# Four stages of a twelve-stage transformer kernel: expert products issued a block ahead, weights quantised two stages early, idle transposes on TensorE, context loads on another queue

## The chip, the cores and the metric

The kernel runs on one core of a Trainium2 chip. The metric is the device time of one launch in microseconds (us); the kernel before was timed three times. All times below are us unless marked ns.

## The reference

The input is x, 32 sequences of 64 tokens of width 128 (2048 tokens in all), a context of 32 sequences of 1601 keys of width 128, and masks over the keys. Four layers follow, each of a cross-attention, a mixer and a feed-forward part; every part adds to x what it computes from a layer norm of x. The change touches three of the twelve parts:

```
L1 ffn, routed experts (8 experts, hidden width 512)
    sim = x e^T; 7 best experts by sim; scores of normalised x and e, + 0.1
    weights = softmax of the two best scores, zero for the other experts
    out = sum over e of weights[e] * (gelu(x W1[e] + b1[e]) W2[e] + b2[e])

L2 xattn, many heads (16 heads of width 8)
    out = softmax(q k^T / sqrt(8), masked keys out) v, then W_o

L3 xattn, one head: softmax((x Wq + bq)(ctx Wk + bk)^T / sqrt(128), masked) (ctx Wv + bv)

L3 ffn, quantised
    Q(m): in blocks of 16, scale = max|m| / 6, |m| / scale rounded to
          the grid 0, .5, 1, 1.5, 2, 3, 4, 6, times sign(m) * scale
    out = Q(silu(Q(x) Q(Wg)^T) * (Q(x) Q(Wu)^T)) Q(Wd)^T
```

## The kernel before

Five engines run programs of their own, written out by hand, and one core does everything. x stays in on-chip memory as 16 tiles of 128 tokens. Each of the twelve parts is one Stage: its buffers live as long as the stage, and at its end all engines meet at a barrier (the profile shows TensorE's side of it as PEq L123). Inside a stage the engines are ordered by semaphores alone. Steps and RoundSteps are lists of step names from which the count is worked out that an engine must wait for, so the order of an engine's work is the order of the code in its block.

**Routed experts** (`routed_experts`). The routing comes first: similarities and norms on TensorE (L1769, L1772), the choice of experts on VectorE, one Exp on ScalarE (L1910), then `weights`, a table of 2048 x 8. TensorE turns it (L1778, 16 transposes) and multiplies it with b2 (L1787, 16 products), which VectorE adds to x. Then come 8 experts by 4 column blocks of 512 tokens, 32 blocks in all. A block is 4 first products of 128x512 (L1800, one for each bank of `ph`), 4 gelus on ScalarE (L1925), 16 second products in four sums of four (L1807, into one of two banks of `po`) and 4 weighted additions to x on VectorE (L1894). The program on TensorE is first, second, first, second. The second products need the block's last gelu, which needs the last of the first products. Every expert's b1 is copied to `b1e` by ScalarE, since the loop's expert index is a register. Weights come on the sync engine's (SP's) queue into two buffers.

**Many heads** (`many_head_cross_attention`). 32 sequences times 14 bundles (each a group of four heads and a part of the keys) give 448 bundles. TensorE's program is a list of steps b from -32 to 457. For b below 0 it prepares keys and values of the first sequences (K at L2975, V at L2971) and, from b = -18, starts the products for the maxima (L2907), 18 bundles ahead of their use (LEAD = 18). In a bundle proper it subtracts the maximum (L2920, L2923), in three bundles of every 14 also takes masked keys out (`less_out`, L2933; in the other eleven VectorE does it with a minimum, L3089), forms the scores (L2894) and three bundles later multiplies with V (L2954). From b = 430 there is nothing left to start for the maxima, and from 448 on only the last sums are finished (L2983 to L2988).

**One head** (`kept_cross_attention`). 16 rounds of two sequences. A round needs the context turned (`ctxT`, 2 x 800 KB), the context (`ctx`, 2 x 800 KB, in four transfers) and the mask, in three buffers each; SP issues them all in one program, mask, turned, then the context of the round before. A turned load waits for the score products of three rounds before (S3), a context load for the products that use it (M3). ScalarE does an Exp of 128x1601 and three copies in a round.

**Quantised layer** (`quantised_ffn`, `Quant`, `quant_vector`, `quant_scalar`). The weights, 128 x 1120 numbers (573 KB), are loaded at the stage's start and quantised by VectorE in 14 instructions (L2520 to L2547), with |y| and the sign of y on ScalarE (L2553 and the line after), y being the weights over their scale. TensorE then turns them (L2606, L2609), and only after copying the result does VectorE begin the layer norm of x. After it come the quantisation of x (`qx`) and, in four groups of 512 tokens, two products, a Silu, the quantisation of the product (`qh`) and the last product. ScalarE's |y| waits for VectorE's y (L2526), and VectorE's next instruction (L2528) waits for |y|.

## Time and profile before

| what | value |
|---|---|
| time, median of 3 | 3136.5 us (3125.68, 3136.5, 3137.94) |
| the profiled execution's own time | 3132.72 us |
| its span, mean granted TensorE clock | 3130.9 us, 0.905 |
| busy | PE 2645.0 (84%), PEld 1692.3, DVE 2029.6 (65%), ACT 1385.4 (44%), POOL 426.2 (14%) |
| DMA | 188.98 MB, mean 60 GB/s |
| largest groups | DVE L3043 544.7, PE L2907 496.4, PE L2894 463.5 (all many heads) |

PE is TensorE's products, PEld its weight loads, DVE VectorE, ACT ScalarE, POOL GpSimd, SP the sync engine, which mostly issues transfers. Busy shares are means over twelve stages with different limits. The stages' places in the span: routed experts 710.8 to 1015.2, many heads 1015.2 to 2262.1, one head 2646.2 to 2826.1 with a self-attention behind it, quantised layer from 2928.3 to the end. The granted clock is a share of 2.4 GHz: 1.00 is that level, 0.50 is the lower level of 1.2 GHz. The profiled execution is 3.8 us below the median.

### The profile page before, as it was taken

To read this page: it belongs to the slowest core of one execution; us is meant where nothing else is said; L and a number is where in the kernel's file an instruction comes from. 1 tells how busy PE (TensorE), PEld (TensorE's weight loads), DVE (VectorE), ACT (ScalarE), POOL (GpSimd) and SP (SyncE) were. 2 spreads that over 40 slices of the span, in tenths; PEclk is the share of its full clock that TensorE was granted. 3 is DMA by queue.
4 is the path that set the end of the run, shared out by engine and by line. 5 is a ranking of instruction groups with operands and counts; after the bars stand their busy time and mean duration, and the time that the engine had idled before them with its cause. 6 is when DMAs were issued, how large, how long until landed. Compare 5 with 4: busy or idle time off the path is not lost. (4 is left out here: it accounts for less than half of the span.)

```text
span 3130.9 us, 65894 instructions
## 1 busy us (share of the span) xinstructions
PE 2645.0 (84%) x26698; PEld 1692.3 (54%) x26698; DVE 2029.6 (65%) x6809; ACT 1385.4 (44%) x2527; POOL 426.2 (14%) x299
## 2 busy tenths in 40 slices
PE   7989555996998799999999999999847988988333
PEld 5767354554666355566555665555525555655223
DVE  5563324674111378999998999889468876436776
ACT  3441222663333145555555555555339953335411
POOL 0000120530000000000000000000006940544100
PEclk9989776997999589999999999999679999999766
DMA  7960420000000100000100001000012211990000
GB/s 247 332 209 1 134 58 7 2 3 15 21 14 9 38 33 23 23 23 23 33 23 23 23 23 33 23 23 2 9 30 68 95 41 52 332 335 9 8 0 14
DMA packets 73343, 188.98 MB, mean 60 GB/s; under 512 B 12130, under 2 KB 39717, under 8 KB 73008
## 3 DMA queue, kind: packets, MB, share of 16 engines
q1 hardware_dynamic: 72016, 182.91, 17.7%
q8 instruction: 212, 3.47, 0.5%
q0 software_dynamic: 1024, 1.85, 0.2%
q14 instruction: 91, 0.75, 0.1%
HBM read 154.19 MB, written 30.79 MB: 59 GB/s over the span
## 5 line engine op out<-in xcount | busy, mean ns | idle before, releaser
L3043 DVE CUSTOM_DVE_ANT_0 L_xattn_junk<-L_xattn_ps_mx,L_xattn_shift 128x512 f32<-128x512 f32 (+1 forms) x1024 | 544.7, 569 | 127.3 <-issue 117.8
L3124 ACT ACTIVATE L_xattn_pT<-L_xattn_ps_st 128x512 f32<-128x512 f32 x768 | 416.9, 594 | 412.4 <-PE L_xattn_ps_st L2894 412.4
L2907 PE MATMUL L_xattn_ps_mx<-L_xattn_kT,L_xattn_qb 32*128 32x512 f32 (+1 forms) x2048 | 496.4, 567 | 1.8 <-DVE L_xattn_tops L3043 1.8
L2894 PE MATMUL L_xattn_ps_st<-L_xattn_qb,L_xattn_kT 32*128 32x256 f32 (+1 forms) x3328 | 463.5, 389 | 0.0
L3089 DVE TENSOR_TENSOR L_xattn_pT<-L_xattn_pT,L_xattn_capT 128x512 f32<-128x512 f32 (+1 forms) x704 | 419.2, 636 | 40.5 <-ACT L_xattn_pT L3124 37.8
L2894 PEld LDWEIGHTS L_xattn_ps_st<-L_xattn_qb,L_xattn_kT 32*128 32x128 f32 (+1 forms) x3328 | 304.1, 183 | 20.6 <-issue 1.2
L2954 PE MATMUL L_xattn_ps_pv<-L_xattn_pT,L_xattn_v 128*17 128x128 f32 x6656 | 267.6, 280 | 0.0
L2954 PEld LDWEIGHTS L_xattn_ps_pv<-L_xattn_pT,L_xattn_v 128*17 128x17 f32 x6656 | 148.4, 98 | 167.0 <-issue 81.0
L2920 PE MATMUL L_xattn_ps_st<-L_xattn_less,L_xattn_ones_b 3*128 3x512 bf16 x768 | 180.7, 390 | 1.4 <-ACT L_xattn_pT L3124 1.2
L1894 DVE SCALAR_TENSOR_TENSOR x<-L_ffn_ps_o,L_ffn_weights,x 128x128 f32<-128x128 f32 x128 | 36.1, 344 | 224.2 <-PE L_ffn_ps_o L1807 224.2
L2907 PEld LDWEIGHTS L_xattn_ps_mx<-L_xattn_kT,L_xattn_qb 32*128 32x128 f32 x2048 | 157.8, 188 | 36.0 <-DVE L_xattn_tops L3043 23.5
L2861 POOL TENSOR_TENSOR L_xattn_qb<-ln_sq,L_xattn_four 128x256 f32<-128x256 f32 x32 | 19.6, 614 | 1105.1 <-PE L_xattn_ps_st L2894 1085.9
L1925 ACT ACTIVATE L_ffn_gelu<-L_ffn_ps_h,L_ffn_b1e 128x512 f32<-128x512 f32 x128 | 87.9, 687 | 163.1 <-PE L_ffn_ps_h L1800 159.7
L1807 PEld LDWEIGHTS L_ffn_ps_o<-L_ffn_w,L_ffn_gelu 128*128 128x128 f32 x1024 | 116.7, 192 | 51.4 <-ACT L_ffn_gelu L1925 51.4
L1807 PE MATMUL L_ffn_ps_o<-L_ffn_w,L_ffn_gelu 128*128 128x128 f32 x1024 | 122.8, 278 | 24.9 <-ACT L_ffn_gelu L1925 24.9
L2971 PE MATMUL L_xattn_ps_prep<-L_xattn_wv,L_xattn_ctxT 128*128 128x128 f32 (+1 forms) x832 | 132.2, 300 | 2.3 <-ACT L_xattn_kT L3137 2.3
L2975 PE MATMUL L_xattn_ps_prep<-L_xattn_ctxT,L_xattn_wk 128*128 128x512 f32 (+1 forms) x256 | 130.1, 592 | 3.1 <-ACT L_xattn_v L3140 2.0
L2971 PEld LDWEIGHTS L_xattn_ps_prep<-L_xattn_wv,L_xattn_ctxT 128*128 128x128 f32 (+1 forms) x832 | 105.2, 196 | 40.4 <-issue 33.1
L2920 PEld LDWEIGHTS L_xattn_ps_st<-L_xattn_less,L_xattn_ones_b 3*128 3x128 bf16 x768 | 45.3, 91 | 135.4 <-ACT L_xattn_pT L3124 75.5
L1800 PE MATMUL L_ffn_ps_h<-xnT,L_ffn_w 128*128 128x512 f32 x256 | 117.2, 601 | 0.0
L2242 ACT ACTIVATE L_attn_xs<-L_attn_xiT,L_attn_bt 128x256 f32<-128x256 f32 x256 | 105.2, 493 | 0.0
L3431 POOL TENSOR_SCALAR L_xattn_out_keys<-L_xattn_mask 128x1536 bf16<-128x1536 uint8 x16 | 78.7, 4919 | 184.6 <-DMA L_xattn_mask<-in_mask_pairs 168.6
(612 smaller groups left out, 4952.9 us busy)
## 6 DMA issues: line engine op xcount, KB each, us to landing
...
L_xattn_out_keys<-scratch_q SPq DMA_DIRECT2D x32, 200.1 KB, 10.0
L_ffn_w<-in_L_ffn_w SPq DMA_DIRECT2D x4, 1024.0 KB, 10.5
...
```

The lines of the kernel that those rows point to most:

```text
L1800: nc.tensor.matmul(ph[:, k, :], w1[:, u, P * k:P * k + P], c.xnT[:, 512 * i:512 * i + 512], start=True, stop=True).then_inc(PE.did(f"h{i}{ ...
L1807: last = nc.tensor.matmul(po[:, i % 2, P * j:P * j + P], g[:, i % 2, k, P * j:P * j + P], w2[:, u, k, :], start=(k == 0), stop=(k == FC - 1))
L2242: last = nc.scalar.mul(xs[:, k % 2, j, :], xiT[:, t, :], bt[:, t, n:n + 1])
L2894: last = nc.tensor.matmul(st[0:chunk[j], w % 3, 256 * c2:256 * c2 + 256], kT[n % 3][r:r + 32, P * j:P * j + chunk[j]], qb[n % 3][r:r + 32, ...
L2907: last = nc.tensor.matmul(mx[:, w % 3, to:to + width], qb[n % 3][32 * g:32 * g + 32, 2 * (p % 2):2 * (p % 2) + 2, :].rearrange("p h q -> p ...
L2920: nc.tensor.matmul(st[:, w % 3, :], ones_b[r:r + 3, :], less[n % 2][r:r + 3, :, :].rearrange("p c k -> p (c k)"), start=True, stop=False, ...
L2954: last = nc.tensor.matmul(pv[32 * q:32 * q + 17, P * half:P * half + P], v[n % 3][0:chunk[j], j, 4 * half + q, :], pT[b % HELD][0:chunk[j] ...
L2971: last = nc.tensor.matmul(prep[0:chunk[j], to:to + P], ctxT[:, n % 2, P * j:P * j + chunk[j]], wv[:, :], start=True, stop=True)
L2975: last = nc.tensor.matmul(prep[:, 0:width], wk[:, :], ctxT[:, n % 2, 512 * m:512 * m + width], start=True, stop=True)
L3043: last = nc.vector.tensor_tensor_reduce(out=junk[:, w % 3, to:to + width], in0=mx[:, w % 3, to:to + width], in1=shift[:, k0:k0 + width], s ...
L3089: nc.vector.tensor_tensor(x, x, capT[0:k, j[0]:j[1], :].unsqueeze(2).broadcast_to([k, j[1] - j[0], 4, S]), ALU.min)\
L3124: nc.scalar.activation(pT[b % HELD][:, :, gi, :], st[:, w % 3, :].rearrange("p (c k) -> p c k", c=2), ACT.Exp)\
```

## The change

1. **Routed experts.** The blocks are numbered n = 0 to 31. TensorE issues the first products of block n+1 ahead of the second products of block n. The two steps that need `weights` (its turns and the products with b2) become `second_bias` and stand ahead of the second products of block 2; so the first products of blocks 0 to 3 and the second of 0 and 1 stand before it. ScalarE does the gelus of blocks 0 to 2 before the routing's Exp. The products with b2 go to the banks of `turn`. All indices are constants, and b1e with its copies is gone.
2. **Many heads, lead-in and end.** `kept_busy(b)` puts transposes of the identity, whose result nobody reads, behind each step of TensorE's program: 8 in each of the 14 steps -32 to -19, 6 in each of the 18 steps -18 to -1, 4 in each of the 27 steps 431 to 457, the last ones behind one wait at b = 431. Masked keys in the last 18 bundles (three with `less_out` before) are left to VectorE.
3. **One head.** The context loads move from SP's queue to ScalarE's: 12 transfers ahead of its layer norm, and four behind its copies in each of the rounds 1 to 13. SP keeps the masks and the turned loads.
4. **Quantised weights.** They get buffers that live over the last three stages. SP issues their load in the one-head stage's round 1; ScalarE takes |w| and sign(w) in round 3; VectorE does one step of the quantisation in each of the rounds 3 to 15. In the quantised layer TensorE's turns start at once.
5. **Quant.** ScalarE takes |m| and sign(m) of the source itself, not of y, and VectorE multiplies |m| by 1/scale in place; the buffer y is gone.

```diff
@@ routed_experts, tensor engine
-                        for k in range(FC):
-                            ...
-                            nc.tensor.matmul(ph[:, k, :], w1[:, u, P * k:P * k + P], c.xnT[:, 512 * i:512 * i + 512],
-                                             start=True, stop=True).then_inc(PE.did(f"h{i}{k}"), 1)
-                        pe.wait_ge(*A.at(f"g{i}{FC - 1}", e))
...
+            first(0)
+            for n in range(BLOCKS):
+                if n + 1 < BLOCKS:
+                    first(n + 1)
+                if n == AHEAD - 1:
+                    second_bias()
+                second(n)
@@ routed_experts, scalar engine
+            act.wait_ge(loaded, 80)
+            for n in range(AHEAD):
+                gelu(n)
             act.wait_ge(*V.at("gap"))
             nc.scalar.activation(ex[:, :], gap[:, :], ACT.Exp).then_inc(A.did("exp"), 1)
...
+            for n in range(AHEAD, BLOCKS):
+                gelu(n)
@@ many_head_cross_attention
-        masked_here = lambda b: b % ROUND in ON_TENSOR
+        masked_here = lambda b: b % ROUND in ON_TENSOR and b < BUNDLES - LEAD
...
+            def kept_busy(b):
+
+                if b < 0:
+                    for _ in range(8 if b < -LEAD else 6):
+                        nc.tensor.transpose(st[:, 2, 0:P], c.ident[:, :], c.ident[:, :])
+                elif b > BUNDLES - LEAD:
+                    if b == BUNDLES - LEAD + 1:
+                        pe.wait_ge(topped, 2 * BUNDLES)
+                    for _ in range(4):
+                        nc.tensor.transpose(mx[:, 0, 0:P], c.ident[:, :], c.ident[:, :])
@@ kept_cross_attention, sync engine, then vector and scalar engine
-                if r >= 1:
-                    if r >= 4:
-                        sp.wait_ge(*PE.at(f"M3_{r - 4}"))
-                    load_context(r - 1)
+                if r == 1:
+                    sp.dma_start(ahead.w[:, :], a[f"{ahead_name}_w"]).then_inc(ahead.loaded, 16)
...
+                quantised_ahead(c, dve, ahead, r)
...
+            for r in range(3):
+                load_context(r)
             ln_scalar(c, act, V, A, PE, tp)
...
+                if 1 <= r < NT - 2:
+                    load_context(r + 2)
+                if r == FIRST_AHEAD:
+                    act.wait_ge(ahead.loaded, 16)
+                    nc.scalar.activation(ahead.q.ay[:, :], ahead.w[:, :], ACT.Abs).then_inc(ahead.signed, 1)
+                    nc.scalar.activation(ahead.q.sign[:, :], ahead.w[:, :], ACT.Sign).then_inc(ahead.signed, 1)
@@ quant_vector, quant_scalar, quantised_ffn
-    nc.vector.tensor_tensor(blocks(q.y[:, :]), blocks(src), wide(q.rscale), ALU.mult).then_inc(*step("y"))
     dve.wait_ge(*A.at(f"{tag}_abs", t))
+    nc.vector.tensor_tensor(blocks(q.ay[:, :]), blocks(q.ay[:, :]), wide(q.rscale), ALU.mult).then_inc(*step("ay"))
...
-    act.wait_ge(*V.at(f"{tag}_y", t))
-    nc.scalar.activation(q.ay[:, :], q.y[:, :], ACT.Abs).then_inc(A.did(f"{tag}_abs"), 1)
-    nc.scalar.activation(q.sign[:, :], q.y[:, :], ACT.Sign).then_inc(A.did(f"{tag}_sign"), 1)
+    c.nc.scalar.activation(q.ay[:, :], src, ACT.Abs).then_inc(A.did(f"{tag}_abs"), 1)
+    c.nc.scalar.activation(q.sign[:, :], src, ACT.Sign).then_inc(A.did(f"{tag}_sign"), 1)
...
-            pe.wait_ge(*V.at("w_out"))
...
-            dve.wait_ge(loaded, 16)
-            quant_vector(c, dve, qw, V, A, "w", 0, w[:, :], w[:, :])
```

`quantised_ahead` holds the same arithmetic as quant_vector, a step for each round:

```
    step = r - FIRST_AHEAD                      # FIRST_AHEAD = 3
    0: scale = max|w|      1: scale / 6         2: 1 / scale
    3: |w| * (1/scale)     4: a = 2 (|y| > 5), b = |y| > 1.75
    5, 6: a += |y| > 3.5, 2.5                   7, 8, 9: b += |y| > 1.25, 0.75, 0.25
    10: a += b / 2         11: a *= sign        12: w = a * scale
```

The order of TensorE's program from the end of the routing's products, before (L1778 and L1787 turn the weights and multiply b2, L1800 are first products, L1807 second):

```order
L1772 MATMUL L_ffn_ps_turn<-L_ffn_emb,L_ffn_ones 128x8
L1778 MATMUL L_ffn_ps_turn<-ident,L_ffn_weights 8x128 x16
L1787 MATMUL L_ffn_ps_o<-L_ffn_b,L_ffn_weightsT 128x128 x16
L1800 MATMUL L_ffn_ps_h<-xnT,L_ffn_w 128x512 x4
L1807 MATMUL L_ffn_ps_o<-L_ffn_w,L_ffn_gelu 128x128 x16
```

And now (L1782 are first products, L1792 second, L1802 and L1811 the weights' turns and b2):

```order
L1773 MATMUL L_ffn_ps_turn<-L_ffn_emb,L_ffn_ones 128x8
L1782 MATMUL L_ffn_ps_h<-xnT,L_ffn_w 128x512 x8
L1792 MATMUL L_ffn_ps_o<-L_ffn_w,L_ffn_gelu 128x128 x16
L1782 MATMUL L_ffn_ps_h<-xnT,L_ffn_w 128x512 x4
L1792 MATMUL L_ffn_ps_o<-L_ffn_w,L_ffn_gelu 128x128 x16
L1782 MATMUL L_ffn_ps_h<-xnT,L_ffn_w 128x512 x4
L1802 MATMUL L_ffn_ps_turn<-ident,L_ffn_weights 8x128 x16
L1811 MATMUL L_ffn_ps_turn<-L_ffn_b,L_ffn_weightsT 128x128 x16
L1792 MATMUL L_ffn_ps_o<-L_ffn_w,L_ffn_gelu 128x128 x16
```

16 first products and 32 second ones now stand between the norms and the weights' turns, and a block's second products have the next block's first products ahead of them.

The lead-in of the many-head stage on TensorE, before (K at L2975, V at L2971, products for the maxima at L2907):

```order
L2975 MATMUL L_xattn_ps_prep<-L_xattn_ctxT,L_xattn_wk 128x65
L2971 MATMUL L_xattn_ps_prep<-L_xattn_wv,L_xattn_ctxT 65x128
L2907 MATMUL L_xattn_ps_mx<-L_xattn_kT,L_xattn_qb 128x512 x2
L2975 MATMUL L_xattn_ps_prep<-L_xattn_ctxT,L_xattn_wk 128x512
L2907 MATMUL L_xattn_ps_mx<-L_xattn_kT,L_xattn_qb 128x512 x4
```

And now (L3002 are the idle transposes, L2982, L2978 and L2914 the three of before):

```order
L2982 MATMUL L_xattn_ps_prep<-L_xattn_ctxT,L_xattn_wk 128x65
L3002 MATMUL L_xattn_ps_st<-ident 128x128 x16
L2978 MATMUL L_xattn_ps_prep<-L_xattn_wv,L_xattn_ctxT 65x128
L3002 MATMUL L_xattn_ps_st<-ident 128x128 x40
L2914 MATMUL L_xattn_ps_mx<-L_xattn_kT,L_xattn_qb 128x512 x2
L2982 MATMUL L_xattn_ps_prep<-L_xattn_ctxT,L_xattn_wk 128x512
L3002 MATMUL L_xattn_ps_st<-ident 128x128 x6
L2914 MATMUL L_xattn_ps_mx<-L_xattn_kT,L_xattn_qb 128x512 x2
```

Nothing of before has moved there; the transposes stand between, 112 ahead of the first product for the maxima and 108 behind it.

A round of the one-head stage on ScalarE now (L3602 is the Exp, L3608 the copies, DMA rows its new issues; before, only the first two stood here, and the four DMA rows stood on SP between the turned loads and the next mask):

```order
L3602 ACTIVATE L_xattn_sc,L_xattn_rows<-L_xattn_sc,L_xattn_bias 128x1601 [waits L3_xattn_vector_steps]
L3608 COPY L_xattn_probsT<-L_xattn_ps_turn 128x512 [waits L3_xattn_tensor_steps] x3
L3590 DMA L_xattn_ctx<-in_ctx 128x1536
L3592 DMA L_xattn_ctx<-in_ctx 65x128
L3590 DMA L_xattn_ctx<-in_ctx 128x1536
L3592 DMA L_xattn_ctx<-in_ctx 65x128
```

The next round's Exp stands behind the four issues.

## Rows read from the trace of the kernel before

**Rows 1.** Stretches: length; busy (instructions) of PE, PEld, DVE, ACT, POOL; clock; DMA share, GB/s
```profile
1042.10:1117.50 75.40, 69.18 (x165) 30.37 (x165) 23.42 (x128) 9.75 (x19) 0.00 (x0) 0.50 0.06 22
...
2676.00:2678.00 2.00, 2.00 (x8) 0.59 (x6) 1.59 (x4) 0.00 (x0) 0.00 (x0) 0.50 0.13 40
2760.00:2770.00 10.00, 8.17 (x87) 5.68 (x85) 3.78 (x20) 3.18 (x5) 5.44 (x3) 1.00 1.02 344
```

**Rows 2.** Timeline of PE, expert loop: start, length, engine, line, output<-inputs, records, [idle before <-releaser]
```profile
861.17 3.60 PE L1800 MATMUL L_ffn_ps_h<-xnT,L_ffn_w 128*128 128x512 f32 x8
865.55 3.84 PE L1807 MATMUL L_ffn_ps_o<-L_ffn_w,L_ffn_gelu 128*128 128x128 f32 x32 [0.78 <-ACT L_ffn_gelu L1925]
869.22 3.60 PE L1800 MATMUL L_ffn_ps_h<-xnT,L_ffn_w 128*128 128x512 f32 x8
```

**Rows 3.** Timeline of PE, routed experts, from the norms to the first block
```profile
729.53 0.57 PE L1772 MATMUL L_ffn_ps_turn<-L_ffn_emb,L_ffn_ones 128*128 128x8 f32 x2
745.00 3.46 PE L1778 MATMUL L_ffn_ps_turn<-ident,L_ffn_weights 128*8 128x128 f32 x16 [14.89 <-DVE L_ffn_weights L1877]
...
754.47 5.62 PE L1800 MATMUL L_ffn_ps_h<-xnT,L_ffn_w 128*128 128x512 f32 x8
```

**Rows 4.** Timeline of ACT, the same stretch
```profile
742.76 0.22 ACT L1910 ACTIVATE L_ffn_ex<-L_ffn_gap 128x16 f32<-128x16 f32 x1 [8.25 <-DVE L_ffn_gap L1860]
...
756.65 1.28 ACT L1925 ACT_TABLE_LOAD   x1 [7.35 <-PE L_ffn_ps_h L1800]
```

**Rows 5.** Timeline of PE, lead-in of the many-head stage
```profile
1042.12 2.08 PE L2975 MATMUL L_xattn_ps_prep<-L_xattn_ctxT,L_xattn_wk 128*128 128x512 f32 x2 [1.11 <-ACT L_xattn_capT L3114]
1044.87 2.07 PE L2971 MATMUL L_xattn_ps_prep<-L_xattn_wv,L_xattn_ctxT 128*128 128x128 f32 x8 [0.68 <-ACT L_xattn_kT L3137]
...
1060.23 2.08 PE L2907 MATMUL L_xattn_ps_mx<-L_xattn_kT,L_xattn_qb 32*128 32x512 f32 x4
```

**Rows 6.** Timeline of PE, idle transposes that the L0 ffn stage already has (L1569)
```profile
393.43 3.91 PE L1569 MATMUL L_ffn_ps_h<-ident 128*128 128x128 f32 x20 [27.40 <-DMA scratch_in<-xn,L_ffn_to]
397.18 1.04 PE L1576 MATMUL L_ffn_ps_turn<-ident,L_ffn_slots 128*128 128x128 f32 x8
```

**Rows 7.** Timeline of PE, end of the many-head stage
```profile
2205.93 0.46 PE L2920 MATMUL L_xattn_ps_st<-L_xattn_less,L_xattn_ones_b 3*128 3x512 bf16 x2
...
2225.06 0.61 PE L2920 MATMUL L_xattn_ps_st<-L_xattn_less,L_xattn_ones_b 3*128 3x512 bf16 x2
...
2228.29 0.61 PE L2920 MATMUL L_xattn_ps_st<-L_xattn_less,L_xattn_ones_b 3*128 3x512 bf16 x2
...
2254.85 2.76 PE L2954 MATMUL L_xattn_ps_pv<-L_xattn_pT,L_xattn_v 128*17 128x128 f32 x48
```

**Rows 8.** Timeline of DVE, the weights' quantisation: its first and its last instruction
```profile
2932.17 1.32 DVE L2520 TENSOR_REDUCE L_ffn_qw_scale<-L_ffn_w 128x70 f32<-128x1120 f32 x1 [4.12 <-DMA L_ffn_w<-in_L_ffn_w]
...
2947.85 1.32 DVE L2547 TENSOR_TENSOR L_ffn_w<-L_ffn_qw_a,L_ffn_qw_scale 128x1120 f32<-128x1120 f32 x1
```

**Rows 9.** Waits of the last 206 us: who waits for whom, us, times, longest
```profile
DVE L_ffn_qh_a L2528 <- ACT L_ffn_qh_ay L2553: 5.8, 4, 1.4
...
DVE L_ffn_qx_a L2528 <- ACT L_ffn_qx_ay L2553: 2.0, 1, 2.0
```

**Rows 10.** Timeline of SP (its issues), one-head stage
```profile
2654.46 0.44 SPq L3408 DMA_DIRECT2D L_xattn_ctx<-in_ctx  x1
...
2760.59 1.33 SPq L3408 DMA_DIRECT2D L_xattn_ctx<-in_ctx  x1
2761.96 3.22 SPq L3410 DMA_DIRECT2D L_xattn_ctx<-in_ctx  x1
2765.22 0.82 SPq L3408 DMA_DIRECT2D L_xattn_ctx<-in_ctx  x1
2766.09 1.19 SPq L3410 DMA_DIRECT2D L_xattn_ctx<-in_ctx  x1
...
2770.58 1.74 SPq L3408 DMA_DIRECT2D L_xattn_ctx<-in_ctx  x1
```

More of the change, by code:

```diff
@@ L1772, in _ @@
             nc.tensor.matmul(tp[1][:, 0:E], ones[:, :], emb2[:, :], start=True, stop=True).then_inc(PE.did("te"), 1)
-            pe.wait_ge(*V.at("weights"))
-            for i in range(4):
-                if i >= 2:
-                    pe.wait_ge(*(A if i % 2 else V).at(f"wT{i - 2}"))
-                for j in range(4):
-                    last = nc.tensor.transpose(tp[i % 2][0:E, P * j:P * j + P], weights[:, 4 * i + j, :], c.ident[:, :])
-                last.then_inc(PE.did(f"wT{i}"), 1)
@@ L2567, in quantised_ffn @@
         nc, a = c.nc, c.a
-        w = s.sb("w", [P, 2 * IP + I])
+        w = ahead.w
         wguT = s.sb("wguT", [P, 2, IP])
```

252 lines of the change are left out of this document (152 added, 100 removed).

## The prediction, made before the changed kernel had run

> **What bounds the kernel now.** Read the stretches first [rows 1]: engines, granted clock and DMA show a different limit in each stage. In the lead-in of the many-head stage TensorE is busy for 69.18 of 75.40 us at clock 0.50: it is the bound, at half speed. In the one-head stage, in ten us, DMA is saturated (share 1.02, 344 GB/s) while VectorE works 3.78 and ScalarE 3.18: transfers are the bound. Then read the timelines. In the expert loop TensorE is the bound but for a wait of 0.78 for the last gelu in each block [rows 2]; before the loop it idles 14.89 for the routing's table [rows 3]. In the quantised layer VectorE works through the weights from 2932.17 to 2949.17 (2947.85 + 1.32), 4.12 after it began to wait for them [rows 8], and everything stands behind it. The waits between engines come last [rows 9]. So all five parts of the change lie on the path, and each is priced in its own stage.
>
> **Expert loop.** A block takes 8.05 (861.17 to 869.22), of which the second products, started at 865.55, take 3.67 [rows 2]. The first products take 8 records of 0.43 = 3.44. With them a block ahead, the gelu runs beside 3.67 of second products and the wait of 0.78, with 0.16 of draining, goes: 7.11 a block. Now the start. The last product of the norms ends at 730.1 [rows 3]. There blocks 0 to 3's first and 0 and 1's second products begin at once, the first block at the low clock (5.4, by the 5.62 at 754.47 [rows 3]), the others 3.44 and 3.67: 5.4 + 3 x 3.44 + 2 x 3.67 = 23.0, end 753.1. The routing on VectorE runs beside it. Its Exp was at 742.76 and the table ready at 745.00, 2.2 later [rows 3, 4]. Now ScalarE still has gelus to do until about 747, then a table load of 1.28 [rows 4], so the table comes at about 750.5, still covered. The turns and the products with b2 took 9.5 (745.00 to 754.47), partly at the low clock; I take 8. Then 30 second and 28 first products: 30 x 3.67 + 28 x 3.44 = 206.4. I add 2.1 for block 2's and 3's sums, which on VectorE stand behind four b2 additions, and 2 for a slower clock after it (5.62 against 3.44 is 2.2). End: 753.1 + 8 + 2.1 + 206.4 + 2 = 971.6. Before it was 754.47 + 2.2 + 32 x 8.05 = 1014.3. **-42.7**, 29 of it from the 31 waits of 0.94, 14 from the start. Bounds: -29 if the start gains nothing, -47 without the two additions. The weights' transfers of an expert have four blocks to land in; the eight copies of b1 went beside TensorE.
>
> **Lead-in of the many heads.** Two halves: preparation from 1042.12 to 1060.23, 18.1, with waits of 0.68 between units [rows 5], and the rest to 1117.50, 57.3, all at 0.50 [rows 1]. A transpose costs 0.20 in the row of 20 at the low clock (3.91) and 0.13 in the next, 8 in 1.04 [rows 6]; that row ends warm, so for one at the low clock I take 0.24, a little under twice 0.13. First half now: a key unit of 2.0 and the first two groups of eight (3.4) at or near the low clock, then five units at 1.04, two of 0.35, and 12 groups of eight at 1.04, which fill the waits: 5.4 + 5.2 + 0.7 + 12.5 = 23.8, **+5.7**. Second half at full clock: 57.3 / 2 = 28.6, plus 18 x 6 x 0.13 = 14.0, is 42.6, **-14.7**. The first bundles, which before still ran at the low clock, give 1: **-10** in all. Bounds: -15 (57.3 + 18.1 halved, plus 28.6 of transposes, less waits filled) and 0, if the clock falls back for a part of it.
>
> Here a rule and a row disagree. The row: 20 transposes of the identity, alone after 27.40 of idling, were followed by transposes at 0.13 each [rows 6], so the clock rose under transposes. The Trainium skill, page "TensorE: Matmul & The Clock Gate", section "Part 4: PE-mode transpose", says that the full clock does not engage for transposes, which do not count as busy in the way products do. By that rule the added work would be pure loss, the rival R2 below, and the sum 3104 in place of 3046. I go by the row, with a doubt: in that stretch a DMA ran too, and in the lead-in products mixed with waits stayed at 0.50 although TensorE was busy 92% of the time.
>
> **End of the many heads.** From b = 431 at 2205.93 to the last sums at 2254.85 is 48.9 [rows 7]. The first bundles take 1.8, then the clock is low and a bundle takes 3.23 (2225.06 to 2228.29), with `less_out` 4.5 to 5. Now, warm: 13 bundles of 1.82, four short ones of 1.23, 17 x 4 transposes of 0.13 (8.8), and about 2 of waiting for a gap in ScalarE or for VectorE's minimum: 39.4. Ten more steps add 5.2 of transposes, which lie in the waits of the last sums, at a doubled speed: +1.3. **-8.** Bounds: -14 without the waits, and +15, the case R1.
>
> **Quantised layer.** The stage started its wait at 2928.05 (2932.17 - 4.12), and the weights were out at 2949.17 [rows 8]: 21.1, less 0.3 for what now has to start cold, -20.8. VectorE's waits for |y| were 2.0 for x and 5.8 in four groups [rows 9]; |m| is now taken beside the block maxima: -7.8. **-28.6.** Bounds: -25 to -29.
>
> **One head.** VectorE's 13 steps of at most 1.32 [rows 8] and ScalarE's two of some 1.2 fit into rounds of 10, in which they are busy 3.8 and 3.2 [rows 1]. On ScalarE 12 issues stand ahead of the layer norm: 12 x 0.44 [rows 10] = +5.3. The context's third load, which waited on SP behind a turned load, now fills the hole at 2676 (40 GB/s [rows 1]): 1.64 MB at 344 GB/s is 4.8, less what moved in it: -4.6. The weights add 573 KB, 1.7. **+2.4.** Behind each round's copies ScalarE issues four transfers, and who waits for that is its next Exp. On SP the four took 1.33 + 3.22 + 0.82 + 1.19 = 6.56 in a round of 9.99 (2760.59 to 2770.58) [rows 10]. ScalarE has 10.0 - 3.2 = 6.8 for them, 1.7 each. That hides them, but by little. I take them to be shorter there, near the 0.44, since SP's queue held mask and turned loads too. Bounds: -4 to +34.
>
> **Sum:** -42.7 - 10 - 8 - 28.6 + 2.4 = -86.9, against the profiled execution's own 3132.7: 3045.8, say **3046**. By the median of the runs, 3.8 higher, it would be 3050.
>
> **The rivals.**
> - **R1, the clock falls at the end of the many heads.** A bundle with waits for ScalarE may lose it as at 2215. Then 22 steps pay 4 x 0.24 = 21, five pay 0.5, three `less_out` (1.5 each) go: +15 to +17 instead of -8. About 3070. For it: TensorE waits for ScalarE's exps and the clock did fall there. Against: the transposes fill just these waits. 0.16.
> - **R2, the lead-in stays at 0.50.** 220 transposes of 0.24 are 53, less 5 for the waits they fill: +48 instead of -10, 3104. For it: 69.18 of 75.40 busy at 0.50 [rows 1]. Against: rows 6. 0.08. The rule of the skill's Part 4 gives this case.
> - **R3, ScalarE's queue.** If an issue costs 1.7 to 2.1 there, the start pays 12 x 1.26 = 15 up to 12 x 1.66 = 20 more, and 13 rounds pay 4 x 2.1 - 6.8 = 1.6 each, 21: between +15 and +41, about 3074. For it: SP's own 6.56. 0.13.
> - **R4, slower than before:** the same place, but each of the issues takes 3.22, the dearest of SP's [rows 10]. 13 x (12.9 - 6.8) = 79, and 12 x 2.78 = 33 at the start: 3158. It is slower by over 0.5% from a mean issue of 3.1 on. Against: no round of SP came near. 0.01.
> - **R5, the first change doesn't do what it says:** the second products still find no gelu ready, because ScalarE's four gelus (a wait of their own for the bank that the second products two blocks ago read) start late. 31 x 0.94 = +29, 3075. Against: 3.67 of cover. 0.03.
>
> **How the numbers follow.** The forecast has 0.59; its own range is 3032 to 3064 by the bounds. To hold 8 in 10 I need R1, most of R3 and R5: 3033 to 3084. A measurement of this kernel tells 0.5% (15.7 us) from no change. Every case but R4 is faster by more than that; two of the rivals together (R2 with R3 or R1) come to 3128 to 3132: faster 0.97, same 0.02, slower 0.01.
>
> **What would show it.** In the profile after: blocks of 7.1 in the expert loop with no wait of second products for the gelu, the loop over near 972; clock near 1.0 by the second key unit of the lead-in, which is 66 long instead of 75.4; clock 1.0 up to the last bundles and the stretch from b = 431 at 39; the last stage shorter by 28; rounds of the one-head stage still 10 long, the issues on ScalarE near 0.5 each. Wrong: a clock of 0.50 in a stretch with idle transposes, rounds of over 10.5, or an Exp that starts late behind an issue.

## The result, and the profile after

The changed kernel takes 3036.44 us (median of 4, 3033.67 to 3038.92), the kernel before beside it 3131.09 (median of 4). The ratio is 0.9699, 95% interval 0.9668 to 0.9729, so 95 us less. The prediction was 3046 with a range of 3033 to 3084. The profiled execution took 3035.62 with a span of 3033.8, which is 97.1 below the span of before. Each stage is read from the start of its first TensorE row:

| stretch | before | after | difference | predicted |
|---|---|---|---|---|
| everything ahead of the routed experts | 710.8 | 713.1 | +2.3 | 0 |
| routed experts | 305.1 | 261.0 | -44.1 | -42.7 |
| many heads, up to the first key unit | 26.2 | 26.7 | +0.4 | 0 |
| lead-in, first key unit to first bundle | 75.4 | 60.1 | -15.3 | -9 |
| bundles, up to b = 431 | 1088.4 | 1089.7 | +1.3 | -1 |
| b = 431 to the next stage | 56.5 | 46.1 | -10.3 | -8 |
| the two stages between | 383.9 | 385.6 | +1.7 | 0 |
| one head | 179.9 | 176.7 | -3.1 | +2.4 |
| self-attention and quantised layer | 304.8 | 274.7 | -30.0 | -28.6 |

The untouched stages (first and seventh row) moved by +4.0 together, from 1094.7 to 1098.7. In the twelve later kernels below, whose code is the same there, they took 1095.2 to 1099.7: they spread over 4.5, and the kernel before lies below all of them. No run explains that.

**Routed experts.** The start, TensorE's timeline (columns as in [rows 2]):

```profile
733.28 9.01 PE L1782 MATMUL L_ffn_ps_h<-xnT,L_ffn_w 128*128 128x512 f32 x16
...
756.14 1.04 PE L1802 MATMUL L_ffn_ps_turn<-ident,L_ffn_weights 128*8 128x128 f32 x8
...
759.30 5.99 PE L1811 MATMUL L_ffn_ps_turn<-L_ffn_b,L_ffn_weightsT 8*128 8x128 f32 x32 [0.76 <-ACT L_ffn_weightsT L1936]
767.23 5.54 PE L1792 MATMUL L_ffn_ps_o<-L_ffn_w,L_ffn_gelu 128*128 128x128 f32 x32 [1.94 <-DVE x L1905]
...
776.05 3.73 PE L1792 MATMUL L_ffn_ps_o<-L_ffn_w,L_ffn_gelu 128*128 128x128 f32 x32
779.62 3.60 PE L1782 MATMUL L_ffn_ps_h<-xnT,L_ffn_w 128*128 128x512 f32 x8
783.05 3.73 PE L1792 MATMUL L_ffn_ps_o<-L_ffn_w,L_ffn_gelu 128*128 128x128 f32 x32
```

The wait of 14.89 for the routing's table [rows 3] is gone: the weights' turns begin at 756.14 without a wait. The wait for the gelu [rows 2] is gone too, and a block takes 7.00 (776.05 to 783.05) in place of 8.05. One new wait stands where the prediction put it: the second products of block 2 wait 1.94 for x0, behind the b2 additions. The clock falls ahead of it, beside the products with b2 (stretches, columns as in [rows 1]):

```profile
758.00:762.00 4.00, 3.24 (x23) 2.94 (x22) 1.46 (x3) 3.39 (x5) 0.00 (x0) 0.82 0.00 0
762.00:766.00 4.00, 3.29 (x16) 2.99 (x15) 1.97 (x3) 0.89 (x2) 0.00 (x0) 0.50 0.00 0
```

**Lead-in of the many heads.** TensorE's timeline, and the first stretch:

```profile
1000.76 1.12 PE L2982 MATMUL L_xattn_ps_prep<-L_xattn_ctxT,L_xattn_wk 128*128 128x512 f32 x2 [1.11 <-ACT L_xattn_capT L3133]
1001.72 1.91 PE L3002 MATMUL L_xattn_ps_st<-ident 128*128 128x128 f32 x16
...
1019.18 1.13 PE L2914 MATMUL L_xattn_ps_mx<-L_xattn_kT,L_xattn_qb 32*128 32x512 f32 x4
...
1060.86 0.39 PE L2927 MATMUL L_xattn_ps_st<-L_xattn_less,L_xattn_ones_b 3*128 3x512 bf16 x2
```

```profile
1000.70:1004.00 3.30, 3.24 (x23) 2.71 (x24) 0.00 (x0) 0.59 (x2) 0.00 (x0) 1.00 0.00 0
```

A key unit is the product of 128x512 that makes keys (L2982). The first one, before any idle transpose, takes 1.12 where it took 2.08 [rows 5]: the clock was at 1.00 when the lead-in began, so the unit at the low clock that the prediction had put in did not have to be paid. The kernel before missed that by little. A product of its stage shortly ahead of the lead-in ran as fast as the changed kernel's, and the clock was at 1.00 up to 0.5 us before its first key unit (timeline, then stretch):

```profile
1038.19 1.02 PE L2877 MATMUL L_xattn_ps_prep<-xnT,L_xattn_wq 128*128 128x512 f32 x2
```

```profile
1031.50:1041.60 10.10, 7.19 (x41) 4.17 (x39) 4.57 (x11) 3.21 (x8) 1.51 (x3) 1.00 0.00 0
```

**Bundles.** They took 1.3 more, though their first ones ran at full clock now. Shortly before b = 431 the clock fell for some 7 us; at the same place of the kernel before it stayed up (after, then before):

```profile
2129.40:2136.10 6.70, 5.96 (x42) 3.12 (x41) 4.96 (x18) 1.64 (x4) 0.00 (x0) 0.50 0.00 0
2184.00:2191.00 7.00, 6.15 (x57) 3.42 (x57) 7.00 (x24) 2.65 (x5) 0.00 (x0) 1.00 0.00 0
```

**End of the many heads.** The whole stretch from b = 431 on ran at 1.00:

```profile
2150.60:2196.70 46.10, 45.55 (x569) 30.53 (x566) 24.56 (x50) 17.71 (x36) 0.00 (x0) 1.00 0.01 1
```

**One head.** ScalarE's timeline in a round (ACTq are its issues), which answers to SP's in [rows 10]:

```profile
2691.23 0.34 ACTq L3590 DMA_DIRECT2D L_xattn_ctx<-in_ctx  x1
2691.31 0.60 ACT L3608 COPY L_xattn_probsT<-L_xattn_ps_turn 128x512 f32<-128x512 f32 x1
2691.61 0.42 ACTq L3592 DMA_DIRECT2D L_xattn_ctx<-in_ctx  x1
2692.06 0.37 ACTq L3590 DMA_DIRECT2D L_xattn_ctx<-in_ctx  x1
2692.46 0.43 ACTq L3592 DMA_DIRECT2D L_xattn_ctx<-in_ctx  x1
2692.93 1.63 ACT L3602 ACTIVATE L_xattn_sc<-L_xattn_sc,L_xattn_bias 128x1601 f32<-128x1601 f32 x1 [1.02 <-issue]
```

Four issues cost 1.56, not SP's 6.56; rivals R3 and R4 are out. The next Exp follows 1.02 later, behind the issues, in a round of 10.2; ten of the 16 Exps were held up so, by 10.8 in all. That was one of the prediction's signs of being wrong. Whether it cost anything, the run with the loads back on SP asks below.

**Quantised layer.** VectorE's layer norm begins at 2863.08 (timeline), 1.7 behind the stage's start at 2861.34. VectorE no longer waits for |m|; of the waits around it one row is left, ScalarE's own for the product (same view as [rows 9]):

```profile
2863.08 0.86 DVE L170 BATCH_NORM_STATS2 ln_stats<-x 128x6 f32<-128x128 f32 x4
```

```profile
ACT L_ffn_qh_ay L2724 <- DVE L_ffn_hh L2682: 2.4, 4, 0.7
```

### The profile page after: what moved, and what is told of

The parts are those of the page before. It is cut to its first block and busy times, and to the rows that moved or that the text cites. A ratio compares the mean times of both kernels' runs of the same rounds, so it can differ in the third digit from the quotient of the medians.

```text
span 3033.8 us, 66495 instructions
## 1 busy us (share of the span) xinstructions
PE 2614.7 (86%) x26984; PEld 1711.9 (56%) x27014; DVE 2036.0 (67%) x6815; ACT 1385.4 (46%) x2520; POOL 429.6 (14%) x299
## 5 line engine op out<-in xcount | busy, mean ns | idle before, releaser
L2914 PE MATMUL L_xattn_ps_mx<-L_xattn_kT,L_xattn_qb 32*128 32x512 f32 (+1 forms) x2048 | 480.0, 551 | 0.0
L2901 PE MATMUL L_xattn_ps_st<-L_xattn_qb,L_xattn_kT 32*128 32x256 f32 (+1 forms) x3328 | 454.5, 383 | 0.0
L2914 PEld LDWEIGHTS L_xattn_ps_mx<-L_xattn_kT,L_xattn_qb 32*128 32x128 f32 x2048 | 151.5, 183 | 23.9 <-DVE L_xattn_tops L3062 14.6
L1926 ACT ACTIVATE L_ffn_gelu<-L_ffn_ps_h,L_ffn_b 128x512 f32<-128x512 f32 x128 | 87.1, 688 | 130.7 <-PE L_ffn_ps_h L1782 127.5
L1792 PEld LDWEIGHTS L_ffn_ps_o<-L_ffn_w,L_ffn_gelu 128*128 128x128 f32 x1024 | 120.8, 194 | 16.6 <-issue 14.1
L2978 PE MATMUL L_xattn_ps_prep<-L_xattn_wv,L_xattn_ctxT 128*128 128x128 f32 (+1 forms) x832 | 124.9, 288 | 0.0
L2982 PE MATMUL L_xattn_ps_prep<-L_xattn_ctxT,L_xattn_wk 128*128 128x512 f32 (+1 forms) x256 | 121.9, 558 | 1.1 <-ACT L_xattn_capT L3133 1.1
L1792 PE MATMUL L_ffn_ps_o<-L_ffn_w,L_ffn_gelu 128*128 128x128 f32 x1024 | 121.1, 277 | 1.9 <-DVE x L1905 1.9
L1782 PE MATMUL L_ffn_ps_h<-xnT,L_ffn_w 128*128 128x512 f32 x256 | 117.0, 600 | 0.0
L2978 PEld LDWEIGHTS L_xattn_ps_prep<-L_xattn_wv,L_xattn_ctxT 128*128 128x128 f32 (+1 forms) x832 | 99.1, 186 | 29.2 <-issue 29.1
## 6 DMA issues: line engine op xcount, KB each, us to landing
L_ffn_w<-in_L_ffn_w SPq DMA_DIRECT2D x4, 1024.0 KB, 10.2
```

Source lines behind the costliest of these rows:

```text
L1782: nc.tensor.matmul(ph[:, k, :], w1[:, e % 2, P * k:P * k + P], c.xnT[:, 512 * i:512 * i + 512], start=True, stop=True).then_inc(PE.did(f"h ...
L1792: last = nc.tensor.matmul(po[:, n % 2, P * j:P * j + P], g[:, n % 2, k, P * j:P * j + P], w2[:, e % 2, k, :], start=(k == 0), stop=(k == F ...
L2901: last = nc.tensor.matmul(st[0:chunk[j], w % 3, 256 * c2:256 * c2 + 256], kT[n % 3][r:r + 32, P * j:P * j + chunk[j]], qb[n % 3][r:r + 32, ...
L2914: last = nc.tensor.matmul(mx[:, w % 3, to:to + width], qb[n % 3][32 * g:32 * g + 32, 2 * (p % 2):2 * (p % 2) + 2, :].rearrange("p h q -> p ...
L2978: last = nc.tensor.matmul(prep[0:chunk[j], to:to + P], ctxT[:, n % 2, P * j:P * j + chunk[j]], wv[:, :], start=True, stop=True)
L2982: last = nc.tensor.matmul(prep[:, 0:width], wk[:, :], ctxT[:, n % 2, 512 * m:512 * m + width], start=True, stop=True)
```

## The experiments

The time lay in the range, but the lead-in lost more than was counted, and its clock was up from the start. That leaves open whether the idle transposes do anything there at all. The first three runs ask this; all experiments start from the changed kernel unless said otherwise.

The kernel before was timed again beside each series of runs, and its median moved from 3130.9 to 3137.1 between them. A time set against the changed kernel's 3036.44 can carry up to 6 us of that. So the readings rest on the lengths of stages in the profiles. Where its code was the same, the routed stage took 260.5 to 261.0, the stretch from b = 431 46.1, and the lead-in 60.1 in six kernels, 61.6 and 61.7 in two. No run undoes the new order of the expert products alone. For it there are only the rows above; the constant indices and the missing b1e copies came with it, and what they are worth isn't separated.

**No idle transposes in the lead-in** (e1)

```diff
                 if b < 0:
-                    for _ in range(8 if b < -LEAD else 6):
+                    for _ in range(0):
```

> The change without the idle transposes of the lead-in (steps below 0). The lead-in is read from the first key unit to the first L2927: 75.4 us before, 60.1 in the changed kernel. Theory 1, the transposes keep the clock up: without them the waits of 0.68 let it fall to 0.50 as before, the lead-in is about 75 and the time +15. Theory 2, in the changed kernel the clock was up at the stage's start for another reason (it stood at 1.00 at the first key unit, before any transpose) and would have stayed: the 220 transposes are then pure cost, the lead-in is 39 (26 of transposes go, 5 of waits come) and the time -21.

Measured: 3047.38 us (ratio to before 0.9723, 0.9698 to 0.9749), 11 more than the changed kernel; lead-in 71.9. TensorE's timeline and two stretches:

```profile
1001.71 1.13 PE L2982 MATMUL L_xattn_ps_prep<-L_xattn_ctxT,L_xattn_wk 128*128 128x512 f32 x2 [1.11 <-ACT L_xattn_capT L3133]
1003.51 1.70 PE L2978 MATMUL L_xattn_ps_prep<-L_xattn_wv,L_xattn_ctxT 128*128 128x128 f32 x8 [0.68 <-ACT L_xattn_kT L3156]
1005.88 2.08 PE L2982 MATMUL L_xattn_ps_prep<-L_xattn_ctxT,L_xattn_wk 128*128 128x512 f32 x2 [0.68 <-ACT L_xattn_v L3159]
```

```profile
1001.70:1008.00 6.30, 4.90 (x12) 2.20 (x12) 0.00 (x0) 1.18 (x3) 0.00 (x0) 0.68 0.00 0
...
1014.00:1020.00 6.00, 4.89 (x16) 3.08 (x16) 0.00 (x0) 1.14 (x4) 0.00 (x0) 0.50 0.12 18
```

The same first unit at full speed (1.13), then a fall within the second, and 2.08 from the third on, but for some 3 us at full clock from 1024.4. Theory 1 holds: the transposes keep the clock up. Theory 2 (39 us) is refuted. But 71.9 is 3.5 less than the 75.4 of before, without a single transpose. So of the 15.3 gained in the lead-in, the transposes account for 11.8; the rest is the clock that happened to be up at the start, and for those 3 us.

The transposes also raise it. Two kernels below (e3, e8) have the changed kernel's code here and yet met the first key unit at the low clock, like the kernel before. TensorE's timeline in e8:

```profile
1001.47 2.07 PE L2990 MATMUL L_xattn_ps_prep<-L_xattn_ctxT,L_xattn_wk 128*128 128x512 f32 x2 [1.11 <-ACT L_xattn_capT L3141]
1003.34 2.58 PE L3010 MATMUL L_xattn_ps_st<-ident 128*128 128x128 f32 x16
1005.76 1.06 PE L2986 MATMUL L_xattn_ps_prep<-L_xattn_wv,L_xattn_ctxT 128*128 128x128 f32 x8
```

Behind 16 transposes the next unit ran at full speed, and the lead-in took 61.7 (61.6 in e3). The low start costs 1.6.

**Half of them** (e4)

```diff
-                    for _ in range(8 if b < -LEAD else 6):
+                    for _ in range(4 if b < -LEAD else 3):
```

> The change with half the idle transposes in the lead-in (4 and 3 a step in place of 8 and 6). If they are enough to keep the clock up: 110 transposes of 0.11 to 0.13 go, 13 us, and some 2 of waits are open again: the lead-in 49 in place of 60.1, time -11. If they aren't: clock 0.50, the lead-in 75 + 110 x 0.24 less the waits they fill, about 97, time +37. If theory 2 of the first run holds, 49 as well.

Measured: 3025.9 us (0.9652, 0.9624 to 0.9681), 11 less than the changed kernel; lead-in 51.5, its clock still full:

```profile
1004.00:1020.00 16.00, 15.05 (x94) 10.18 (x92) 3.89 (x18) 3.25 (x7) 0.00 (x0) 1.00 0.16 52
1020.00:1050.50 30.50, 30.50 (x156) 15.69 (x154) 19.50 (x111) 5.32 (x11) 0.00 (x0) 1.00 0.08 28
```

Half are enough, and the other half cost 8.6 us, less than the expected 11: waits of 0.24 between the units are open again.

**Four in the preparation, none behind it** (e11)

```diff
-                    for _ in range(8 if b < -LEAD else 6):
+                    for _ in range(4 if b < -LEAD else 0):
```

> The change with 4 idle transposes in each step from -32 to -19 (preparation, where waits of 0.68 stand between the units) and none from -18 on, where TensorE works without a wait. The lead-in took 60.1 with 8 and 6, 51.5 with 4 and 3, 71.9 with none. Theory 1: it is the waits that let the clock fall; held through the preparation it stays: the lead-in takes 51.5 - 54 x 0.125 = 45, time -14 against the changed kernel. Theory 2: the products of narrow tiles from -18 on don't hold the clock by themselves: it falls to 0.50 there, and the lead-in takes some 70.

Measured: 3029.32 us (0.9673, 0.9657 to 0.9689); lead-in 55.3, between both theories. TensorE's timeline behind step -18, and two stretches:

```profile
1033.06 1.62 PE L2914 MATMUL L_xattn_ps_mx<-L_xattn_kT,L_xattn_qb 32*128 32x512 f32 x6
1034.97 2.35 PE L2914 MATMUL L_xattn_ps_mx<-L_xattn_kT,L_xattn_qb 32*128 32x512 f32 x10 [0.29 <-DVE L_xattn_tops L3062]
1037.84 3.67 PE L2914 MATMUL L_xattn_ps_mx<-L_xattn_kT,L_xattn_qb 32*128 32x65 f32 x12 [0.52 <-DVE L_xattn_tops L3062]
```

```profile
1020.00:1030.00 10.00, 10.00 (x43) 4.38 (x42) 5.78 (x26) 2.99 (x6) 0.00 (x0) 1.00 0.00 0
1030.00:1050.00 20.00, 19.19 (x58) 9.17 (x57) 12.38 (x79) 1.49 (x4) 0.00 (x0) 0.62 0.13 42
```

At first the products kept the clock by themselves, from 1013.6 on for some 21 us. It fell at 1034.9, ahead of the products of 32x65 and of the wait of 0.52. In the 5.5 us before, TensorE had products for the maxima (32 rows) and two short units (65 columns) and no full unit of keys or values, and a wait of 0.29 at the end. Which of these did it isn't separated.

**No idle transposes at the end** (e2)

```diff
-                    for _ in range(4):
+                    for _ in range(0):
                         nc.tensor.transpose(mx[:, 0, 0:P], c.ident[:, :], c.ident[:, :])
```

> The change without the idle transposes of the stage's end (steps 431 to 457); masked keys stay on VectorE there. Read from b = 431 to the next stage: 56.5 before, 46.1 in the changed kernel. Theory 1, the transposes keep the clock up: without them it falls some 10 us into the stretch, bundles take 3.2, and the stretch takes 51 to 53, time +6. Theory 2, the clock is kept because less_out and its wait are gone: it stays up, and the stretch loses the transposes as well: 46.1 - 27 x 0.59 = 30, with some waits 33, time -13.

Measured: 3040.24 us (0.9699, 0.9674 to 0.9723); the stretch 52.7, that is +6.6. The clock is low again (columns as in [rows 1]):

```profile
2170.00:2180.00 10.00, 10.00 (x82) 5.74 (x80) 4.01 (x7) 3.26 (x6) 0.00 (x0) 0.50 0.01 2
```

Theory 1: the stretch lies in the expected range. Leaving masked keys to VectorE doesn't keep the clock up.

**Masked keys on TensorE again** (e3)

```diff
-        masked_here = lambda b: b % ROUND in ON_TENSOR and b < BUNDLES - LEAD
+        masked_here = lambda b: b % ROUND in ON_TENSOR
```

> The change with masked keys of bundles 438, 441 and 443 on TensorE again; the transposes stay. Theory 1 (transposes keep the clock): three groups of 0.5 to 0.9 more, the stretch from b = 431 at 48, time +2. Theory 2 (less_out with its wait lets the clock fall): the stretch takes 60 or more, with bundles of 3.2 and transposes at the low clock, time +15.

Measured: 3040.11 us (0.9693, 0.9662 to 0.9725; single times from 3031 to 3045, so that the time alone tells nothing here); the stretch 48.4, +2.3, at full clock:

```profile
2170.00:2180.00 10.00, 10.00 (x126) 6.30 (x122) 3.57 (x8) 4.34 (x8) 0.00 (x0) 1.00 0.00 0
```

Again theory 1: the three groups cost their own time and no more. Of the 10.3 gained at the end, 2.3 are thus the masked keys'; without the transposes only 3.8 (56.5 to 52.7) would be left.

**Context loads back on SP** (e6)

```diff
@@ sync engine
+                if r >= 1:
+                    if r >= 4:
+                        sp.wait_ge(*PE.at(f"M3_{r - 4}"))
+                    load_context(r - 1)
...
@@ scalar engine
-            for r in range(3):
-                load_context(r)
             ln_scalar(c, act, V, A, PE, tp)
...
-                if 1 <= r < NT - 2:
-                    load_context(r + 2)
```

> The change with the context loads back on SP's queue, in the order of before (the weights' load stays on SP in round 1, and so does the quantisation ahead). The one-head stage took 179.9 before and 176.7 in the changed kernel. Theory 1 (the prediction's): the move costs 5.3 ahead of the layer norm and gives 4.6 at the hole; undone, the stage takes 176. Theory 2: two queues keep the transfers denser throughout; undone, the stage takes 179.9 + 1.7 for the weights = 181.5, time +5.

Measured: 3036.7 us (0.9701, 0.9684 to 0.9717); the stage 177.2, against 176.7 with the loads on ScalarE. Nothing is seen of theory 2's 181.5, and the Exps that start behind issues cost nothing that shows. But the stage took 176.6 to 180.6 in the eleven kernels in which its code was that of the change, so a difference of one or two microseconds can't be told here, nor can the 3.1 between before and after. What the move does change is the price of an issue: the 64 context issues of the stage took 1.18 each on average here, 1.20 in the kernel before, and 0.44 on ScalarE.

**Weights in the quantised stage** (e10)

```diff
@@ quantised_ffn
...
+            dve.wait_ge(ahead.loaded, 16)
+            quant_vector(c, dve, ahead.q, V, A, "w", 0, w[:, :], w[:, :])
             dve.wait_ge(*PE.at("wgT"))
...
@@ kept_cross_attention
-                quantised_ahead(c, dve, ahead, r)
...
```

> The change with the weights loaded and quantised in the quantised stage again (|w| of the source, so without VectorE's wait of 1.2). Theory 1: the 13 steps were hidden in the one-head stage but for the transfer of 1.7: the last stage +20, the one-head stage -1.7, time +18. Theory 2: the steps cost time in the rounds too (VectorE was busy 5.0 to 5.6 of ten us there, 3.8 before): the one-head stage shorter by 4 or more, time +16 or less.

Measured: 3054.24 us (0.9756, 0.974 to 0.9772), 18 more. The self-attention and quantised layer take 293.8 in place of 274.7, +19.0 unrounded; the one-head stage 173.4, which is 3.3 less than in the changed kernel and 3.2 to 7.2 less than in the eleven kernels with its code. Theory 1 has the size of the gain. That the weights' work in the one-head stage was hidden but for 1.7 is doubtful: it costs 3 or more, and theory 2's 4 fits as well.

**|y| in place of |m|** (e9)

```diff
-    dve.wait_ge(*A.at(f"{tag}_abs", t))
-    nc.vector.tensor_tensor(blocks(q.ay[:, :]), blocks(q.ay[:, :]), wide(q.rscale), ALU.mult).then_inc(*step("ay"))
-    then("ay")
+    nc.vector.tensor_tensor(blocks(q.y[:, :]), blocks(src), wide(q.rscale), ALU.mult).then_inc(*step("ay"))
+    dve.wait_ge(*A.at(f"{tag}_abs", t))
...
@@ quantised_ffn, scalar engine
-                    act.wait_ge(*V.at("h3", r - 1))
-                    nc.scalar.activation(qh.ay[:, :], flat(hh), ACT.Abs).then_inc(*A.inc("h_abs"))
...
+                    act.wait_ge(*V.at("h_ay", r))
+                    nc.scalar.activation(qh.ay[:, :], qh.y[:, :], ACT.Abs).then_inc(*A.inc("h_abs"))
...
```

> The change with ScalarE taking |y| and sign(y) of the scaled y again, for x and for the four groups (the weights ahead as in the change). From the layer norm's start to the end the quantised layer took 178.9 before and 170.7 in the changed kernel. Theory 1 (the prediction's): VectorE waits again 2.0 once and 1.4 four times, 7.8 in all: 178.5, time +8. Theory 2: ScalarE, which has the Abs and Sign off its path at another time now, is what shortened the groups; with the old order the waits return only in part: 174, time +3 to +4.

Measured: 3045.57 us (0.9702, 0.9685 to 0.972). That is 9 more than the changed kernel, but against the kernel before beside it the ratio is the same (0.9699), so the time doesn't show the loss; the stage does. From the layer norm's start (2868.73) to the end (3047.5) it is 178.8, against 170.7; expected were 178.5. The waits are those of [rows 9], to the tenth:

```profile
DVE L_ffn_qh_a L2541 <- ACT L_ffn_qh_ay L2723: 5.8, 4, 1.4
DVE L_ffn_qx_a L2541 <- ACT L_ffn_qx_ay L2564: 2.0, 1, 2.0
```

**Less cover for the routing** (e7)

```diff
-        BLOCKS, AHEAD = 4 * E, 3
+        BLOCKS, AHEAD = 4 * E, 1
```

> The change with AHEAD = 1: first products still a block ahead, but the weights' turns and b2 products stand ahead of the second products of block 0, so that only two blocks' first products cover the routing in place of four's first and two's second. The routed stage took 261.0 in the changed kernel. Theory 1: the table comes at 749 to 750 (no gelus of block 2 in ScalarE's way), TensorE runs dry at 742 and waits 7; the wait for x0 (1.94) and its slow second products (+1.8) go: 264 to 266, time +3 to +5. Theory 2: the whole start is worth what the prediction said (14 over waiting for the table): 270 or more.

Measured: 3043.76 us (0.9696, 0.9679 to 0.9714; again the ratio of the changed kernel, and the stage is what tells); the routed stage 267.9, +6.9, between both theories. TensorE's timeline:

```profile
746.94 3.66 PE L1802 MATMUL L_ffn_ps_turn<-ident,L_ffn_weights 128*8 128x128 f32 x16 [6.03 <-DVE L_ffn_weights L1889]
751.35 7.16 PE L1811 MATMUL L_ffn_ps_turn<-L_ffn_b,L_ffn_weightsT 8*128 8x128 f32 x32 [0.76 <-ACT L_ffn_weightsT L1936]
758.44 5.87 PE L1792 MATMUL L_ffn_ps_o<-L_ffn_w,L_ffn_gelu 128*128 128x128 f32 x32
```

The table came earlier (746.9, since ScalarE has fewer gelus ahead of the Exp) and the wait is 6.03. What I had left out is the clock: after that wait the turns take 3.66, the products with b2 7.16 and the second products 5.87, where the changed kernel has 1.04 twice, 5.99 and 5.54.

**Sums of blocks 0 and 1 early** (e8)

```diff
             nc.vector.tensor_tensor(weights[:, :, :], part1[:, :, :], part2[:, :, :], ALU.add).then_inc(V.did("weights"), 1)
+            weighted(0)
+            weighted(1)
             for i in (0, 2):
...
```

> The change with VectorE's sums of blocks 0 and 1 (x0, x1) right behind the routing's table, ahead of the copies of the turned weights and the b2 additions. The routed stage took 261.0 in the changed kernel. Theory 1: the second products of block 2 wait 1.94 only for x0 behind the b2 additions, and run at 0.50 (5.54 in place of 3.73) only because of it: 257 to 258, time -3 to -4. Theory 2: the clock falls already with the waits for the copies at 757.5 and 759.3: 259, -2. Theory 3: the sums delay the first copy, and what is gained is lost: 261.

Measured: 3035.7 us (0.9692, 0.9676 to 0.9708); the routed stage 259.9, -1.1. TensorE's timeline:

```profile
761.00 5.92 PE L1811 MATMUL L_ffn_ps_turn<-L_ffn_b,L_ffn_weightsT 8*128 8x128 f32 x32 [0.76 <-ACT L_ffn_weightsT L1944]
766.85 6.57 PE L1792 MATMUL L_ffn_ps_o<-L_ffn_w,L_ffn_gelu 128*128 128x128 f32 x32
```

The wait of 1.94 is gone, and the second products, now without any, take 6.57: the clock was down already, as theory 2 said, and more of the 1.94 is given back than it allowed. It falls beside the products with b2, as in the changed kernel (758 to 762 above). Ahead of them stand waits of 0.34 and 0.76 for copies, and the products themselves have 8 rows; which of the two lets the clock fall, this run doesn't separate.

**A candidate from these** (e12): half the idle transposes in the lead-in, 2 in place of 4 at the end, the sums early, and the products with b2 apart:

```diff
                 if n == AHEAD - 1:
                     second_bias()
+                if n == AHEAD:
+                    biases((2, 3))
                 second(n)
+                if n == AHEAD - 1:
+                    biases((0, 1))
...
```

> A candidate: the change with 4 and 3 idle transposes in the lead-in, 2 in place of 4 at the end, x0 and x1 ahead of the b2 additions, and the products with b2 behind the second products of block 2 (two of them) and behind the first products of block 4 (the other two), so that VectorE's and ScalarE's copies and additions lie beside products. Expected: lead-in 51.5 (-8.6); the end -27 x 2 x 0.13 = -5 if the clock holds with half of them (+6 if not, as without any); routed stage 261.0 - 6 = 255 if the clock doesn't fall there any more, 258 if it does. Time 3036 - 20 = 3016, or 3028.

Measured: 3014.18 us (0.9605, 0.959 to 0.9619): 22 less than the changed kernel, with intervals of the ratios that don't meet. Expected were 3016 or 3028. Routed stage 254.8, lead-in 51.5, end 41.2. TensorE's timeline and stretch in the routed stage:

```profile
757.12 3.74 PE L1793 MATMUL L_ffn_ps_o<-L_ffn_w,L_ffn_gelu 128*128 128x128 f32 x32
760.79 2.05 PE L1814 MATMUL L_ffn_ps_turn<-L_ffn_b,L_ffn_weightsT 8*128 8x128 f32 x16
762.77 3.70 PE L1783 MATMUL L_ffn_ps_h<-xnT,L_ffn_w 128*128 128x512 f32 x8
```

```profile
757.00:773.00 16.00, 16.00 (x110) 12.96 (x108) 5.20 (x12) 7.03 (x10) 0.00 (x0) 1.00 0.01 1
```

The b2 products lie between wide ones, in this stretch nothing waits, and the clock stays: the routed stage is 6.2 shorter, where e8 got 1.1. The new order took away the wait of 0.76 together with the run of narrow products, so the two stay unseparated. At the end, half the transposes hold the clock as well (41.2, 5.0 less).

**Fewer still** (e13): the candidate with 2 and 2 transposes in the lead-in and 1 at the end.

```diff
-                    for _ in range(4 if b < -LEAD else 3):
+                    for _ in range(2 if b < -LEAD else 2):
...
-                    for _ in range(2):
+                    for _ in range(1):
```

> The candidate of before with 2 and 2 idle transposes in the lead-in (in place of 4 and 3) and 1 at the end (in place of 2). If the clock holds: lead-in 51.5 - 28 x 0.11 - 18 x 0.13 + waits open again 3 = 49, the end -27 x 0.13 = -3.5 less waits, time 3014 - 5 = 3009. If 0.46 of waiting between units is enough to let it fall, as 0.68 was without any: lead-in 70 to 75, time 3035; if it falls at the end alone: +8, 3022.

Measured: 3037.31 us (0.9683, 0.9662 to 0.9704), 23 more than the candidate. The clock held through the preparation in spite of the waits of 0.46, but fell to 0.66 on average in the 20 us before the first bundle: lead-in 54.7, 3.2 more. At the end it fell for good, and the stretch took 57.6, 16 more than the candidate's and longer than before the change. The 3035 of the case with the waits came out by luck: the loss lies at the end, where 8 were expected, and not in the lead-in.

```profile
2135.00:2148.00 13.00, 13.00 (x177) 7.98 (x173) 8.31 (x31) 7.23 (x15) 0.00 (x0) 1.00 0.00 1
2148.00:2152.00 4.00, 3.92 (x30) 2.71 (x30) 3.14 (x6) 2.17 (x4) 0.00 (x0) 0.82 0.02 4
2152.00:2190.00 38.00, 38.00 (x314) 20.16 (x311) 13.14 (x26) 9.98 (x20) 0.00 (x0) 0.50 0.00 1
```

## Why the prediction was right, and where its steps failed

The time, 3036, lay in the range, 10 below the forecast and 3 above the range's lower end. Against the spans it is -97.1 where -86.9 was worked out. The parts that were priced missed by -14.6 together (lead-in -6.3, one head -5.5, end -2.3, the expert loop and the last row -1.4 each, bundles +2.3), and the stages that nobody had touched gave 4.4 of that back. That the sum lies this close is in part luck.

- **Expert loop, -42.7 against -44.1.** Right in mechanism and size. The block was put at 7.11 and is 7.00, so the 31 blocks give 32.6 where 29 was forecast, and the start 11.5 where 14 was. The table came 40.4 behind the stage's start, not 39.7, and was still under cover; turns and b2 products took 9.1 (756.14 to 767.23 less the wait), not 8; the 2.1 for x0's turn on VectorE was 1.94 and the 2 for the clock 1.8. The run with AHEAD = 1 shows what the cover is worth: with 9.0 us of products in place of 22.9 ahead of the table, the stage is 6.9 longer. R5, second products that still wait for the gelu, didn't happen.
- **Lead-in, -9 against -15.3.** The cause was right: without the transposes the clock falls, with them it is 1.00. Its first half was mis-sized, 23.8 where 18.4 was measured; the second took 41.7, as forecast (42.6). Half of the difference is the start: "a key unit of 2.0 and the first two groups of eight (3.4) at or near the low clock". They took 1.12 and 1.91, and 2.7 from the first start to the end of both, where 5.4 was put, since the clock happened to be up. About 1.5 of that was luck and no effect of the change: the kernels e3 and e8, with the same code, began low, and their lead-in took 1.5 and 1.6 more. The other half is the sum's own. It added up the lengths of rows (1.04 for a group of eight), but a row's end overlaps the next row's start, and from start to start a group took 0.88.
- **The gain of 1 from the first bundles** is covered by something else. In three kernels below, as in the one before, the clock did not fall shortly before b = 431. Their bundles took 1087.2 and 1087.4 where the clock was up at the first bundle (e12, e13), and 1088.2 where it was low there (e1), as in the kernel before (1088.4): a gain of about 1. In the changed kernel and the nine others the clock fell there for 3 to 10 us, and they took 1089.7 to 1091.3. What decides on that fall no run shows; the code is the same.
- **R2** (3104) didn't happen. With 4 and 3 transposes a step the clock is 1.00 throughout, without any it is 0.50 for most of the lead-in. The rule of the Trainium skill, page "TensorE: Matmul & The Clock Gate", section "Part 4: PE-mode transpose", that transposes don't count as busy in the way products do, doesn't agree with these two stretches. The transposes that keep it are of fp32 and 128x128, and the trace prints them as MATMUL rows like any product; no run here tried another type.
- **End, -8 against -10.3.** R1 didn't happen. Up to the last sums it took 37.1 (2150.58 to 2187.70) where 39.4 was forecast: the 2 put in for waits were not needed, since TensorE was busy 45.55 of the whole 46.10. What comes behind cost 1.5 more than before, as forecast (1.3). Masked keys (2.3) and transposes (6.6, by their absence) are both shown. With one transpose a step the clock does fall (57.6, about 1 more than before the change); R1's +15 for four at the low clock was never met.
- **Quantised layer, -28.6 against -30.0.** Two runs show the halves: weights in the stage +19.0 (forecast 20.8, of which that run leaves out a wait of 1.2), |y| +8.1 (forecast 7.8).
- **One head, +2.4 against -3.1.** The sign isn't shown by any run: the spread of the stage between kernels with the same code is 4. The issues in a round cost 0.39 each, near the 0.44 that was taken. The 12 ahead of the layer norm took 7.1, not 5.3 (2582.29 to 2589.39), and the first Exp still came earlier from the stage's start (33.7, before 35.1). The weights' work, put at 1.7, costs 3 or more.
